# A gated cross-attention model on one core: the fifteen inverse square roots move from ScalarE's Ln and Exp to GpSimd's power

## What is computed

```python
def _layernorm(x, axis=-1, eps=1e-05):
    m = jnp.mean(x, axis=axis, keepdims=True)
    v = jnp.var(x, axis=axis, keepdims=True)
    return (x - m) / jnp.sqrt(v + eps)
def _rmsnorm(t):
    return t * jax.lax.rsqrt(jnp.mean(t * t, axis=-1, keepdims=True) + EPS)

x = x + jnp.tanh(g_xattn[0]) * wkv(w, u, layernorm(x), ctx)          
x = x + jnp.tanh(g_ffn[0]) * bitlinear_ffn(layernorm(x), gate, up, down)
x = x + jnp.tanh(g_xattn[1]) * attention(layernorm(x), ctx, Wq, Wk, Wv) 
x = x + jnp.tanh(g_ffn[1]) * experts(layernorm(x), ...)              
```

## Time and profile before

| | us |
|---|---|
| median of 3 runs | 532.3 (531.12 to 532.79) |
| span of the profiled execution | 529.0 |
| that execution's own time | not given apart from its span |
| TensorE matmul busy | 407.7 (77%) |
| VectorE busy | 349.0 (66%) |
| ScalarE busy | 285.0 (54%) |
| GpSimd busy | 49.2 (9%) |

### The profile page before, as it was taken

The page is one execution under the profiler, slowest core; times in us unless marked ns, Lnnn a source line. Parts: engine busy times, 40 slices in busy tenths (PEclk is TensorE's granted clock), DMA queues, the critical chain, the costliest instruction groups (busy, mean ns, idle before and its releaser), DMA issues.

```text
span 529.0 us, 7361 instructions
## 1 busy us (share of the span) xinstructions
PE 407.7 (77%) x2602; PEld 196.1 (37%) x2606; DVE 349.0 (66%) x725; ACT 285.0 (54%) x433; POOL 49.2 (9%) x37
## 2 busy tenths in 40 slices
PE   1001535648667798877799999999999999999994
PEld 1001123325443343433355444444444444444442
DVE  5899599894875655755496576655656566564553
ACT  2845583667787889887455345334343343332321
POOL 0725641002000111000000000000000000000000
PEclk9655756778999889998799999999999999999998
DMA  8300000000002000005520345434334433312211
GB/s 307 162 1 0 1 0 1 1 0 1 0 2 61 1 1 1 2 13 149 156 80 25 100 149 154 151 106 139 114 101 136 130 106 113 125 65 64 76 61 40
DMA packets 23808, 38.27 MB, mean 72 GB/s; under 512 B 3802, under 2 KB 10330, under 8 KB 23260
## 3 DMA queue, kind: packets, MB, share of 16 engines
q1 hardware_dynamic: 23772, 37.80, 22.6%
HBM read 36.48 MB, written 1.31 MB: 71 GB/s over the span
## 4 chain that ended last, share of the span: by engine, by line
PE 56%; DVE 21%; ACT 11%; issue 8%; DMA 3%; POOL 1%; SPq 1%; DVEq 0%; ACTq 0%
PE ps L1128 33%; PE ps L1373 16%; ACT regA L634 3%; DVE regA L789 2%; DVE xn L757 1%; PE ps L1285 1%; DVE regA L778 1%; DMA regA<-in_dp_dram 1%; PE ps L1185 1%; DMA x<-in_x_dram 1%; PE ps L1120 1%; DMA regA<-routing_dram 1%; DVE bn L743 1%; DVE regA L796 1%; PE ps L1191 1%
## 5 line engine op out<-in xcount | busy, mean ns | idle before, releaser
L1128 PE MATMUL ps<-hH,regB 128*128 128x512 f16 x528 | 169.2, 382 | 0.0
L686 ACT ACTIVATE regA<-ps 128x512 f32<-128x512 f32 x66 | 39.4, 597 | 150.4 <-PE ps L1128 150.4
L1086 DVE TENSOR_TENSOR regA<-ps,regA 128x512 f32<-128x512 f32 x66 | 45.6, 691 | 100.9 <-ACT regA L686 100.9
L1128 PE MATMUL ps<-hL,regB 128*128 128x512 f16 x264 | 100.8, 382 | 0.0
L1373 PE MATMUL ps<-regA,regB 128*128 128x512 f16 x396 | 96.3, 379 | 1.3 <-DVE regA L1091 1.3
L1128 PEld LDWEIGHTS ps<-hH,regB 128*128 128x128 f16 x528 | 52.0, 98 | 63.2 <-issue 2.5
L634 ACT ACTIVATE regA<-ps 128x1024 f32<-128x1024 f32 x64 | 62.0, 1025 | 10.0 <-PE ps L1315 9.1
L1373 PEld LDWEIGHTS ps<-regA,regB 128*128 128x128 f16 x396 | 38.6, 98 | 48.5 <-DVE regA L1091 2.3
L1096 DVE TENSOR_TENSOR regA<-regA 128x512 f32<-128x512 f32 x66 | 45.2, 685 | 1.3 <-DMA regA<-routing_dram 1.3
L1091 DVE TENSOR_TENSOR regA<-regA 128x512 f16<-128x512 f32 x66 | 45.0, 682 | 0.7 <-ACT regA L678 0.7
L678 ACT CAST regA<-regA 128x512 f16<-128x512 f32 x66 | 40.2, 610 | 1.5 <-DVE regA L1096 1.5
(11 more groups left out here) (165 smaller groups left out, 510.9 us busy)
## 6 DMA issues: line engine op xcount, KB each, us to landing
regA<-routing_dram SPq DMA_DIRECT2D x132, 128.0 KB, 3.0
regA<-in_gu_dram SPq DMA_DIRECT2D x33, 256.0 KB, 2.6
regA<-in_dp_dram SPq DMA_DIRECT2D x33, 128.0 KB, 2.7
regA<-in_ffn_dram SPq DMA_DIRECT2D x2, 1024.0 KB, 8.3
x<-in_x_dram SPq DMA_DIRECT2D x2, 512.0 KB, 4.0
ctxT<-in_ctxT_dram SPq DMA_DIRECT2D x1, 1024.0 KB, 8.2
regB<-in_ffn_dram SPq DMA_DIRECT2D x1, 1024.0 KB, 12.2
out_dram<-x SPq DMA_DIRECT2D x2, 512.0 KB, 3.4
```

The costliest lines, as they stand in the source:

```text
L686: nc.scalar.activation(sgm[:, c % 2, :], bank(GATE_BANK[c % 2]), ACT.Silu, scale=UNSCALE).then_inc(esilu_done, 1)
L1086: V.tensor_tensor(sgm[:, c % 2, :], bank(GATE_BANK[c % 2] + 1), sgm[:, c % 2, :], ALU.mult).then_inc(et_done, 1)
L1128: mm = T.matmul(out_ap, w(k), a(k), start=(n == 0), stop=(n == 3 * DK - 1))
```

## The change

GpSimd computes each root whole: power -0.5 of ve against a tile of constants mhalf, then the Newton step, five instructions with a wait after each (through the semaphore g_ord, the last through root_ready). VectorE's root_end keeps one multiplication by the gain, into an rstd that now has two buffers. ScalarE's first_root and its calls are removed, with the table loads around them at t = 0, t = 4 and norm 8. GpSimd's program now walks the two tables for its roots too: roots 2 and 3 stand behind differences(3) and ahead of clamp(0) and clamp(1), roots 4 and 5 behind clamp(2), and in attention each root stands in the order of BESIDE among the splits.

```diff
-            def first_root(n):
-                act.wait_ge(var_ready, e + 1)
-                post(nc.scalar.activation(lnv[:, 0:n], ve[:, e % 2, 0:n], ACT.Ln))
-                settle()
-                nc.scalar.activation(root[:, e % 2, 0:n], lnv[:, 0:n], ACT.Exp, scale=-0.5).then_inc(root_ready, 1)
-                act.wait_ge(root_ready, e + 1)
...
+            def beside_roots(tasks):
+                for name, i in tasks:
+                    if name == "stats":
+                        inverse_root(NORM_TILES[i][1] - NORM_TILES[i][0])
+                    elif name == "rows":
+                        inverse_root((ROW_RUNS[i][1] - ROW_RUNS[i][0]) * HEADS)
+                    elif name == "split" and i not in VECTOR_ROWS:
+                        split(i)
...
+            def link(ins):
+                done[0] += 1
+                ins.then_inc(g_ord, 1)
+                pool.wait_ge(g_ord, done[0])
...
+            def inverse_root(n):
...
+                pool.wait_ge(var_ready, e + 1)
+                v, y, t = ve[:, e % 2, 0:n], guess[:, 0:n], newt[:, 0:n]
+                link(nc.gpsimd.tensor_tensor(y, v, mhalf[:, 0:n], ALU.pow))
+                link(nc.gpsimd.tensor_tensor(t, v, y, ALU.mult))
+                link(nc.gpsimd.tensor_tensor(t, t, y, ALU.mult))
+                link(nc.gpsimd.tensor_scalar(t, t, -0.5, 1.5, ALU.mult, ALU.add))
+                nc.gpsimd.tensor_tensor(root[:, e % 2, 0:n], t, y, ALU.mult).then_inc(root_ready, 1)
+                pool.wait_ge(root_ready, e + 1)
+
+            link(nc.gpsimd.memset(mhalf[:, :], -0.5))
+            inverse_root(HT)
+            inverse_root(HT)
             for c in range(4):
                 differences(c)
+            inverse_root(HT)
+            inverse_root(HT * HEADS)
             clamp(0)
             clamp(1)
-            for n in range(2 * TT):
-                if n == HT:
-                    clamp(2)
-                if n not in VECTOR_ROWS:
-                    split(n)
+            for n in range(HT):
+                split(n)
+            clamp(2)
+            inverse_root(HT * HEADS)
+            inverse_root(HT)
+            for n in range(HT, TT):
+                split(n)
+            inverse_root(HT)
+            inverse_root(2 * HEADS)
+            for n in range(NG + 1):
+                beside_roots(BESIDE.get(n, ()))
+            for c in range(NCH + 1):
+                beside_roots(BESIDE_EXPERTS.get(c, ()))
...
-                if t == 0:
-                    nc.scalar.preload_act_table_set(EXP_LN)
-                    first_root(HT * HEADS)
-                    first_root(HT)
-                    nc.scalar.preload_act_table(ACT.Silu)
-                elif t == 4:
-                    nc.scalar.preload_act_table_set(EXP_LN)
-                    first_root(HT)
-                    nc.scalar.preload_act_table(ACT.Silu)
...
-                    if name in ("norm", "weigh"):
+                    if name == "weigh":
                         nc.scalar.preload_act_table_set(EXP_LN)
...
-                v, r = ve[:, e % 2, 0:n], root[:, e % 2, 0:n]
-                dve.wait_ge(var_ready, e + 1)
                 dve.wait_ge(root_ready, e + 1)
-                link(V.tensor_tensor(newt[:, 0:n], v, r, ALU.mult))
-                link(V.tensor_tensor(newt[:, 0:n], newt[:, 0:n], r, ALU.mult))
-                link(V.tensor_scalar(newt[:, 0:n], newt[:, 0:n], -0.5 * gain, 1.5 * gain, ALU.mult, ALU.add))
-                link(V.tensor_tensor(rstd[:, 0:n], newt[:, 0:n], r, ALU.mult))
+                link(V.tensor_scalar(rstd[:, e % 2, 0:n], root[:, e % 2, 0:n], gain, None, ALU.mult))
+                return rstd[:, e % 2, :]
```

More of the change, by code:

```diff
@@ L76, in bass_flamingo @@
         ve = sb("ve", [P, 2, P])
-        lnv = sb("lnv", [P, P])
+        mhalf = sb("mhalf", [P, P])
+        guess = sb("guess", [P, P])
         root = sb("root", [P, 2, P])
         newt = sb("newt", [P, P])
-        rstd = sb("rstd", [P, P])
+        rstd = sb("rstd", [P, 2, P])
         hH = sb("hH", [P, DK, NT], F16)
@@ L406, in split @@
                 nc.gpsimd.tensor_tensor(lo, rows, hi, ALU.subtract).then_inc(repL, 1)
+            def beside_roots(tasks):
[6 more added lines that the diff above has]
+                        split(i)
+            done = [0]
+            def link(ins):
+                done[0] += 1
+                ins.then_inc(g_ord, 1)
+                pool.wait_ge(g_ord, done[0])
+            event = [0]
+            def inverse_root(n):
+                e = event[0]
+                event[0] += 1
+                pool.wait_ge(var_ready, e + 1)
[9 more added lines that the diff above has]
+            inverse_root(HT)
             for c in range(4):
                 differences(c)
+            inverse_root(HT)
+            inverse_root(HT * HEADS)
             clamp(0)
             clamp(1)
-            for n in range(2 * TT):
-                if n == HT:
-                    clamp(2)
-                if n not in VECTOR_ROWS:
-                    split(n)
+            for n in range(HT):
[11 more added lines that the diff above has]
+                beside_roots(BESIDE_EXPERTS.get(c, ()))
         @block.scalar
@@ L427, in settle @@
                 act.wait_ge(a_ord, done[0])
-            event = [0]
-            def first_root(n):
-                e = event[0]
-                event[0] += 1
-                act.wait_ge(var_ready, e + 1)
-                post(nc.scalar.activation(lnv[:, 0:n], ve[:, e % 2, 0:n], ACT.Ln))
-                settle()
-                nc.scalar.activation(root[:, e % 2, 0:n], lnv[:, 0:n], ACT.Exp, scale=-0.5).then_inc(root_ready, 1)
-                act.wait_ge(root_ready, e + 1)
             def abs_sum(m):
@@ L645, in beside @@
                     project(i, bank(6))
-                elif name == "rows":
-                    first_root((ROW_RUNS[i][1] - ROW_RUNS[i][0]) * HEADS)
                 elif name == "split":
                     split(i)
-                elif name == "norm":
-                    first_root(NORM_TILES[i][1] - NORM_TILES[i][0])
                 elif name == "weights":
@@ L752, in norm @@
                 a, b = NORM_TILES[q]
-                root_end(b - a, gain)
+                scale = root_end(b - a, gain)
                 if q in FORMER:
@@ L756, in norm @@
                 for t in range(a, b):
-                    ins = V.tensor_scalar(xn[:, t, :], x[:, t, :], mv[:, t, 0:1], rstd[:, t - a:t - a + 1],
+                    ins = V.tensor_scalar(xn[:, t, :], x[:, t, :], mv[:, t, 0:1], scale[:, t - a:t - a + 1],
                                           ALU.subtract, ALU.mult)
@@ L833, in rows_end @@
                 a, b = ROW_RUNS[r]
-                root_end((b - a) * HEADS, 1.0)
+                scale = root_end((b - a) * HEADS, 1.0)
                 dve.wait_ge(proj_read, b)
@@ L837, in rows_end @@
                     rows = kc[:, n % HT, :].rearrange("p (h d) -> p h d", h=HEADS)
-                    root = rstd[:, (n - a) * HEADS:(n - a + 1) * HEADS]
+                    root = scale[:, (n - a) * HEADS:(n - a + 1) * HEADS]
                     V.tensor_tensor(rows, rows, root.unsqueeze(2).broadcast_to([P, HEADS, HD]),
```

5 lines of the change are left out of this document (removed).

## The result

The kernel after takes 610.9 us at the median (609.9 to 611.5), the kernel before 531.9: a ratio of 1.146, interval 1.141 to 1.151. The forecast was 528.1 in a range of 524 to 538. The whole of it lies before the experts: TensorE's steady stretch (266 to 529 us in the earlier trace rows) begins at 346.2 us instead of 266.2, 80.0 us later, and the span is 80.3 us longer.

What follows compares the result with a forecast made beforehand. TensorE holds 56% of the chain, VectorE 21%; the stretch from 266 us was taken as fixed, so only an earlier expert start counts. Terms 0.9 + 1.3 + 1.55 + 1.3 - 0.85 save 4.2 us: 528.1 us, range 524 to 538.

Steps and rivals of the forecast that it cites:

- the price of the power: GpSimd's power in each root: an estimated 0.3, 0.85 and 1.45 us at 4, 64 and 128 columns.
- The slower rival: Power dear at every width, felt in GpSimd's queue between ve and split: 537.5 us at 2 us each; chance 0.32.
- rule of 6x: An extra x us per root costs 6x from norm 4 through attention; the sign turns at x = 0.7.
- The plain steps: Four GpSimd steps per root besides the power, links included: an estimated 0.65, 1.0 and 1.45 us at 4, 64, 128 columns.
- the sum below: Savings and losses in order of time over the kernel: 0.9 + 1.3 + 1.55 + 1.3 - 0.85 = 4.2 us saved.
- (a): First norms: norm(0) and norm(1) start earlier, then the first scan waits for ScalarE's copy of the keys: 0.9 us saved.
- (b): Around 63 us: rows' product 4.0 us earlier without ScalarE's exponentials ahead, 2.7 given back to moved clamps: net 1.3 saved.
- (c): rows_end(1) and norm(3), 110 to 117 us: VectorE is the chain, both roots ready long before: 1.55 us saved.
- (d): 140 to 158 us: two table loads gone, norm(4) shorter, root of rows 2 on GpSimd: 1.3 us saved.
- (e): Attention: small savings, but 1.6 us lost by splits behind the root of stats(6); together 0.85 us lost.
- A cost at first use: Rival: the first power, on the path at 6.5 us, needs a load of about 6 us: 532 us; chance 0.07.
- Given back: Rival: moved clamps cost VectorE 3.4 us or more, attention pauses lower TensorE's clock: 531 to 533 us; chance 0.09.

Runs made afterwards that it cites:

- e1: The kernel after with the power replaced by a plain product of the same width, roots not computed: 531.8 us, 0.9998 of the kernel before.
- e6: As e1, but clamp(0) and clamp(1) back ahead of roots 2 and 3 on GpSimd: 528.9 us, 0.9896 of the kernel before.
- e5: As e1, but split(12) and split(13) ahead of the root of norm 6 on GpSimd: 532.1 us, 0.9957 of the kernel before.
- e8: All roots computed, GpSimd's power only for norms 0 to 4 and 8, other roots as in the kernel before: 529.2 us, 0.9898 of it.
- e10: All roots computed, GpSimd's power only for norms 2, 3, 4 and 8, everything else as in the kernel before: 528.9 us, 0.9908 of it.
- e9: The kernel before with eight powers of several shapes added on GpSimd behind its last split, nobody waiting for them: 530.5 us, one execution, no ratio.

## Why the prediction was wrong

**The step that failed is the price of the power.** The prediction took an estimated 0.85 and 1.45 us at 64 and 128 columns, "about three or four plain ones", and the dearest two-input row, 3.08 us, as the upper bound. Measured: 10.55 and 20.79. The upper bound was no bound: it was another operation's row, and nothing tied the power to it. The choice had a second fault. It was made as a price per instruction with a small slope (0.009 us a column), while the measured one is nearly all slope, 0.160 us a column against 0.002 for a plain two-input step (0.45 us at 128 columns, 0.32 at 64). On the narrow roots the same estimate was off by only 0.4 to 0.7 us.

**The slower rival named the mechanism**: GpSimd's queue between ve and split, VectorE standing still in rows_end, "a power of about 1.5 us at 64 columns" as the turning point. All of that is what the trace shows; its price of 2 to 3 us was a fifth to a third of the real one at 64 columns and a tenth to a seventh at 128. Its rule of 6x gives 58 us with x = 9.7 at 64 columns, and leaves out the two roots of 128 columns, by which the kernel after lost 18.1 and 11.9 us: the rule took one price for every width.

**The plain steps** were too cheap at every width. The four with their links took 1.04, 1.46 and 1.91 us at 4, 64 and 128 columns (7.45 to 8.49, 195.51 to 196.97 and 85.20 to 87.11 us in the kernel after) where the prediction had 0.65, 1.0 and 1.45; a link is 0.08 us and not 0.05. So the five steps of e1, without a power, took 1.3, 1.8 and 2.4 us, near the prediction's 0.95, 1.85 and 2.9 with one: where e1 meets the sum below, two errors that cancel have a part in it. On wide tiles they took 0.45 us to VectorE's 0.29, and on 4 columns 0.20 to 0.16. The Trainium skill ("GPSIMD Engine Reference", section Engine selection) puts VectorE at about twice GpSimd's speed on two inputs; here it is a factor of 1.25 to 1.6. By that rule the prediction had 1.3 us for the four steps at 4 columns; the 1.04 measured lies between it and 0.65.

**(a)** 0.9 us expected, 1.2 in e1 and 0.35 in the kernel after (first scan at 13.43), where the narrow power of 1.06 us counts. **(b)** 1.3 expected, 0.4 in e1. The moved clamps cost 2.2 us of it (e6) where 2.7 were allowed for; the rest of the miss was not taken apart. That they collide with VectorE was right; that only products of two SBUF inputs suffer was wrong. **(c)** 1.55 expected, 1.5 measured, in e1. In the kernel after, "both roots are ready long before" was wrong by 11.2 us. **(d)** 1.3 expected, 1.2 in e1, with a root of 1.8 us where 1.85 was expected: luck, by the two errors above. **(e)** 0.85 lost expected, 4.1 lost in e1: the place was right (the splits behind the root of norm 6), the size was not, because TensorE waited 4.2 us and then ran at the lower clock. e5 shows it for 2.7 of them; the rest, most of it between rows 2 and rows 4, was not taken apart. That stretch took 14.5 us from rows 2 to rows 3 in the kernel before and 16.4 in e1, but also 14.4 in e8 and 17.3 in e10, which have the same program there.

**Around the span.** The prediction took 3.3 us for what lies around it, 532.3 less 529.0. In the runs whose time and span are both given it is 1.8 us (611.1 and 609.3 in the kernel after); the other 1.5 is that the profiled execution was faster than the median. The forecast does not change by it.

**The other rivals.** A cost at first use: the first power took 1.02 us and the later ones of its width 1.01 to 1.06, so there is none. Given back: that is what e1 shows, with the ratio 0.9998 for the change at a plain price, and it was given 0.09; its two places are right, though the clamps cost 2.2 us and not 3.4. The table loads did go, as the change says: seven are left of thirteen. The experts' stretch was 263.1 us in the kernel after, as forecast.

## What to carry to other kernels

When a change rests on an operation that no row of the trace shows, the nearest row is no upper bound for it; ask what sets its duration, columns or instructions, and let the range take in a slope, or measure the one operation at two widths before anything is built on it. Split such work by width: a power of 4 columns costs 1 us and frees two other engines, a power of 128 costs 21. And when work is moved into an idle engine's queue, list what it now stands ahead of: here the same roots ahead of two clamps cost 2.2 us and one ahead of two splits 2.7 in its stretch, both had back by changing the order.

## What the runs showed that was not expected

GpSimd's power goes by columns, not by partitions: 20.8 us for 128 columns on 1, 16, 64 or 128 partitions.

A clamp on GpSimd (one input, 2048 columns, 1.94 us) holds off even a VectorE instruction of 4 columns with one tile input: line 888 took 1.94 us instead of 0.23, as long as the whole second clamp, and in the kernel after the scaling of rows 0 took 1.95. The Trainium skill ("Advanced Engine Details and Errata", section VectorE Performance Modes) notes that GpSimd and VectorE's two-port instructions "will interfere/block eachother" over a shared port; beside the clamp the traces agree, with blocking for its full length, if line 888 is such an instruction, which no run shows by itself.

Beside the power they don't. In the kernel after, line 888 took its usual 0.23 us at 67.40 us, under the power that ran from 64.33; line 767, at 64.31 us, took 1.60 us instead of 1.38, 0.2 more. In e9 powers filled GpSimd's time from 207 to 310 us (102.7 of 103), and VectorE was busy 65.5 us in this stretch, before 65.8. A VectorE product whose inputs all lie in SBUF, twelve times in it, kernel before and then e9:

```profile
L1096 DVE TENSOR_TENSOR regA<-regA 128x512 f32<-128x512 f32 x12 | 8.2, 685 | 1.3 <-DMA regA<-routing_dram 1.3
```

```profile
L1114 DVE TENSOR_TENSOR regA<-regA 128x512 f32<-128x512 f32 x12 | 8.2, 684 | 3.5 <-DMA regA<-routing_dram 3.5
```

So the power costs whoever waits for it, and hardly anyone beside it.

Behind a pause of TensorE of 4.2 us in attention the granted clock was 0.50 for 5 us, and the turns and weighted values there took 2.0 us more than at 2.4 GHz. With a pause of 1.4 us instead (e5) the stretch from rows 4 to rows 5 was 2.7 us shorter, less than pause and clock added up (2.8 and 2.0): in e5 VectorE waited 2.1 us for the root of norm 6, now behind the splits, and 1.2 in e1.
